# A gather list whose empty places point past the end of the table

## The reference

```
xn  = layernorm(x)
h   = xn @ W
AHW = segment_sum(edge_weight[:, None] * h[dst], src, num_segments=12500)
x   = x + AHW + b + linear_attention(xn)
x   = x + mixture_of_experts(layernorm(x))     # 8 experts, the best 2 for each node
```

## Time and profile before

| | |
|---|---|
| median of 3 runs | 3717.16 us (3711.85 to 3720.75) |
| profiled execution | 3712.03 us |
| its span, first to last instruction | 3710.3 us |
| POOL's gathers at L770 | 1616, 1549.9 us busy |
| HBM read, written | 376.35 MB, 111.03 MB |

### The profile page before, as it was taken

How to read it: one execution, slowest core, us unless ns; L and a number is a source line. 1 busy time by engine, 2 the same in 40 slices (tenths; PEclk the granted TensorE clock), 3 DMA queues, 4 the chain that set the end, 5 groups by cost and what they waited for, 6 DMA issues and landing times. The chain is left out here.

```text
span 3710.3 us, 69265 instructions
## 1 busy us (share of the span) xinstructions
PE 2723.5 (73%) x16161; PEld 2235.5 (60%) x16165; DVE 2553.0 (69%) x6668; ACT 628.5 (17%) x1326; POOL 2548.0 (69%) x2390
## 2 busy tenths in 40 slices
PE   1447776577777777676676667667767999999998
PEld 1346666366566665555555555555533788888887
DVE  9999999455555555677777777777768566654444
ACT  8312222411111111000000000000013221112221
POOL 7347777677777777777777777777745477775444
PEclk9987777789999999888899898998877999999999
DMA  5545555634444444444444444444457455555443
GB/s 173 167 144 183 180 184 158 222 117 128 127 125 128 125 124 126 131 131 125 131 131 131 129 127 131 131 131 124 125 177 220 73 115 114 112 114 92 73 75 52
DMA packets 327621, 492.01 MB, mean 133 GB/s; under 512 B 60714, under 2 KB 247854, under 8 KB 327214
## 3 DMA queue, kind: packets, MB, share of 16 engines
q0 software_dynamic: 127584, 270.17, 28.9%
q1 hardware_dynamic: 161029, 176.37, 15.6%
q10 hardware_dynamic: 38601, 41.04, 3.5%
HBM read 376.35 MB, written 111.03 MB: 131 GB/s over the span
## 5 line engine op out<-in xcount | busy, mean ns | idle before, releaser
L770 POOL DMA_INDIRECT message<-h_table,records x1616 | 1549.9, 959 | 511.5 <-issue 498.4
L1278 PE MATMUL bank<-message,select 128*128 128x256 f32 x3232 | 924.5, 436 | 566.7 <-issue 296.6
L1278 PEld LDWEIGHTS bank<-message,select 128*128 128x128 f32 x3232 | 665.4, 215 | 781.7 <-issue 404.2
L1821 DVE TENSOR_SCALAR select<-iota_n,records 128x128 f32<-128x128 f32 x1660 | 594.3, 358 | 501.4 <-PE bank L1278 486.9
L1829 DVE TENSOR_TENSOR acc<-acc,bank 128x256 f32 x1660 | 683.4, 412 | 9.9 <-PE bank L1278 6.0
L823 POOL DMA_INDIRECT out<-acc,row_of x210 | 331.7, 1580 | 302.5 <-DVE acc L2356 152.5
L735 POOL DMA_INDIRECT lists<-placed,dest_i x300 | 348.5, 1162 | 201.2 <-ACT placed L957 106.9
L1514 PE MATMUL bank<-w,acc 128*128 x1680 | 387.1, 384 | 19.7 <-DVE acc L2340 19.7
L1501 PE MATMUL bank<-fx_t,acc 128*128 128x256 f32 x1680 | 380.1, 379 | 2.5 <-ACT fx_t L1096 2.5
L1514 PEld LDWEIGHTS bank<-w,acc 128*128 128x128 f32 x1680 | 315.6, 193 | 61.5 <-issue 21.5
L1501 PEld LDWEIGHTS bank<-fx_t,acc 128*128 128x128 f32 x1680 | 318.7, 190 | 46.0 <-ACT acc L1103 1.9
(11 more groups left out here) (356 smaller groups left out, 3579.2 us busy)
## 6 DMA issues: line engine op xcount, KB each, us to landing
fetched<-h_table SPq DMA_DIRECT2D x3200, 1.0 KB
fetched<-h_table ACTq DMA_DIRECT2D x2432, 1.0 KB
rows<-block_dram SPq DMA_DIRECT2D x75, 514.5 KB
acc<-x_sorted SPq DMA_DIRECT2D x105, 260.0 KB, 3.1
message<-h_table,records POOLq DMA_INDIRECT x1616
xt_in<-xt_dram SPq DMA_DIRECT2D x98, 256.0 KB
lists<-zeros_list SPq DMA_DIRECT2D x8, 1664.0 KB, 14.9
read_back<-lists SPq DMA_DIRECT2D x13, 1024.0 KB, 7.0
```

Of the source, the lines that this page charges most:

```text
L770: pool.indirect_dma_start(out=message[:, k % SETS, j, :], out_offset=None, in_=h_table, in_offset=Offset(ap=records[:, k * SET + j, 0:1], ...
L1278: last = nc.tensor.matmul(ps, select[:, slot % 2, j, :], rows_of, start=True, stop=True)
L1821: return V.tensor_scalar(select[:, k % 2, j, :], iota_n[:, :], records[:, k * SET + j, 1:2].bitcast(F32), records[:, k * SET + j, 2:3].bit ...
```

## The change

The number that marks a place without an edge is now 16,384 (`ABSENT`), past the last row of `h_table`, and every gather gets a bound, 12,543, with rows above it to be skipped. `message` is zeroed once, so that a slot that has never been written holds zeros; later a skipped place keeps what an earlier set left there, and its weight of 0 takes it out. The row numbers of the tiles that SP and ACT fetch are cut off at 12,543, since those transfers have no bound. The column `lane` and its iota go.

```diff
--- before.py
+++ after.py
@@ -91,6 +91,8 @@
     PAD = 1 << 14
     assert NB * 2 * (G8 - 1) + CG <= SLOTS and K % STEP == 0 and NCOL >= NGP and M % 5 == 0 and TAIL_REST
     SET, SETS, RING = 4, 4, 8
+    ABSENT = 1 << 14
+    assert ABSENT >= NB * P
     TT = -(-((NG * P + NB * (P - 1)) // P) // SET) * SET
     RSEG = -(-TT // P)
     TC = RSEG * P
@@ -250,7 +252,7 @@
         row_ok = sb("row_ok", [P, 2, P], F32, early)
         w_nat = sb("w_nat", [P, 8, C], F32, early)
         message = sb("message", [P, SETS, SET, C], F32, early)
-        lane = sb("lane", [P, 1], F32, early)
+        absent = sb("absent", [P, 1], F32, early)
         select = sb("select", [P, 2, SET, P], F32, early)
         fetched = sb("fetched", [P, 2, 2, C], F32, early)
         fetch_f = sb("fetch_f", [P, FETCHED], F32, early)
@@ -748,7 +750,8 @@
             steps.settle()
             pool.engine_nop().then_inc(s_late, 1)
             pool.iota(iota_n[:, :], [[1, P]], base=0, channel_multiplier=0, allow_small_or_imprecise_dtypes=True)
-            pool.iota(lane[:, :], [[1, 1]], base=0, channel_multiplier=1, allow_small_or_imprecise_dtypes=True)
+            pool.memset(absent[:, :], float(ABSENT))
+            pool.memset(message[:, :, :, :], 0.0)
             steps.done(pool.memset(head_mask[:, :], 1.0))
             steps.done(pool.memset(row_ok[:, :, :], 1.0))
             steps.settle()
@@ -769,7 +772,8 @@
                 for j in range(SET - (k in fetched_of)):
                     pool.indirect_dma_start(
                         out=message[:, k % SETS, j, :], out_offset=None, in_=h_table,
-                        in_offset=Offset(ap=records[:, k * SET + j, 0:1], axis=0)).then_inc(s_message[k % SETS], 16)
+                        in_offset=Offset(ap=records[:, k * SET + j, 0:1], axis=0),
+                        bounds_check=NB * P - 1, oob_is_err=False).then_inc(s_message[k % SETS], 16)
             for k in range(TSETS):
                 pool.wait_ge(s_records, part_of(k))
                 if k >= SETS:
@@ -1879,7 +1883,7 @@
                 steps.done(V.tensor_tensor(records[:, part, 2], fb, fa, ALU.bitwise_or))
                 steps.settle()
 
-                steps.done(V.tensor_scalar(fa, records[:, part, 2].bitcast(F32), 0.0, lane[:, 0:1], ALU.is_equal, ALU.mult))
+                steps.done(V.tensor_scalar(fa, records[:, part, 2].bitcast(F32), 0.0, absent[:, 0:1], ALU.is_equal, ALU.mult))
                 steps.settle()
                 V.tensor_tensor(records[:, part, 0], records[:, part, 0], fa, ALU.max).then_inc(s_records, 1)
                 if nth == 0:
@@ -1896,8 +1900,10 @@
                 for k in (range(1, 3), range(3, 6), range(6, 7), range(0))[nth]:
                     set_turn(k)
             dve.wait_ge(s_records, len(PARTS))
-            steps.done(V.tensor_copy(fetch_f[:, 0:SP_FETCHED], records[:, SP_TILE:SP_TILE + (SP_FETCHED - 1) * SP_SPAN * SET + 1:SP_SPAN * SET, 0]))
-            steps.done(V.tensor_copy(fetch_f[:, SP_FETCHED:FETCHED], records[:, ACT_TILE:ACT_TILE + (ACT_FETCHED - 1) * ACT_SPAN * SET + 1:ACT_SPAN * SET, 0]))
+            steps.done(V.tensor_scalar(fetch_f[:, 0:SP_FETCHED], records[:, SP_TILE:SP_TILE + (SP_FETCHED - 1) * SP_SPAN * SET + 1:SP_SPAN * SET, 0],
+                                       float(NB * P - 1), None, ALU.min))
+            steps.done(V.tensor_scalar(fetch_f[:, SP_FETCHED:FETCHED], records[:, ACT_TILE:ACT_TILE + (ACT_FETCHED - 1) * ACT_SPAN * SET + 1:ACT_SPAN * SET, 0],
+                                       float(NB * P - 1), None, ALU.min))
             steps.settle()
             V.engine_nop().then_inc(s_fetch_f, 1)
             for k in range(RING - 1, RING):
```

## The result

The changed kernel takes 3,798.3 us (median of 4 runs, 3,789.95 to 3,804.63) against 3,714.5 of the kernel before in the same comparison: a ratio of 1.0228, with a 95% interval of 1.0205 to 1.0251. It is slower, by 84 us where 53 were forecast. The profiled execution has a span of 3,796.7 us, 86.4 more than before.

A forecast was written before the change was run, and what follows sets the result against it. POOL's gathers were taken to bound the stage. The profiled 3,712.0 us plus 53 for the bound and 0 for the rest gave 3,765, with 5 us more 3,770 us as a median; range for 8 in 10: 3,635 to 3,960.

The forecast's parts named there:

- What bounds the stage: POOL's 1,616 gathers at L770 set the pace, 1.268 us each; a nanosecond per gather is 1.616 us of the kernel.
- The bound's price: Each gather at L770 compares 128 row numbers with a bound: 33 ns taken, 53 us in all; high end 1,012 us.
- The rows skipped: 12,094 absent places in POOL's gathers needn't be written: between nothing and 89 us saved, nothing taken into the forecast.
- The middle bound: POOL's time per skipped row, from the accumulating scatter's extra 626 ns for 128 rows: 4.9 ns each, 59 us in all.
- The operand: An extra instruction per gather on POOL's sequencer for the bound: hidden, cost 0; uncovered, 17 ns each, 27 us.
- The memset: Zeroing `message` once on POOL before the first gather: 3.5 us, covered by 8.5 us of waiting, cost 0.
- Skipping pays: Rival at L770: bound free, 4.9 ns saved per absent row, 47 us in all, 3,670 us; chance 0.34.
- Nothing changes: Rival at L770: bound compared at no cost, skipped rows still written out in some form, 3,717 us; chance 0.20.
- A pass of its own over the rows: Rival at L770: the check adds 150 to 626 ns per gather, 3,959 to 4,729 us; chance 0.07.
- The sign: Direction of the whole kernel's change: slower 0.46, the same 0.20, faster 0.34.

The follow-up runs named there:

- the shorter list: The kernel before with `TT` smaller by 36 tiles, 35 of them gathered by POOL and all empty on these inputs: 3,667.9 us, ratio 0.9887.
- the run with one move: The changed kernel with the bound moved into a register once ahead of the gathers, instead of once for each of the 1,616: 3,798.8 us, ratio 1.0245.

## Why the prediction was right, and where it was off

*What bounds the stage.* Right. 55.7 ns more per start make 90.0 us over 1,615 steps, the shorter list gave 44.7 us where 44 were expected, and the gathers of 64 and 32 rows took 72 and 122 us off the kernel, where 46 and 83 ns a gather make 74 and 134. With 32 rows the stage of the profile is 127 us shorter (2614.8 - 693.1 against 2,048.3) and the part behind it 10 us longer, which is within what that part varies by.

*The bound's price: the mis-sized term.* I took 33 ns, from the scatter at L805 as the nearest row. The bound alone measures 53, the changed kernel 56. The direction was right for the reason given, extra work in every gather. The size came from a row that has nothing to do with checking, the difference between two directions of transfer; that it lies within a factor of two is luck. With 56 ns in its place the sum is 3,717 + 90 = 3,807, 9 us above the 3,798 measured. 3 of them are the kernel before, which has 3,714.5 in this comparison; the rest lies within what the part behind the last gather varies by. What the work is stays open: the runs show that a bound lengthens each gather whether or not a row is skipped, and without the moves, but they don't separate the comparing of 128 row numbers from whatever else the instruction does when it has a bound.

*The rows skipped.* Nothing was taken for them and nothing came: 998 ns with half of all rows skipped. The middle bound, 4.9 ns per row from the accumulating scatter, was wrong by four to seven times for a row that the instruction hasn't got (0.7 to 1.2 ns), and altogether for one that it has and skips. The 626 ns of that scatter therefore aren't the price of 128 more rows of this kind; what they are was not tried. The rule of the Trainium skill that was weighed against them ("DMA: Bandwidth & Descriptors", on the anatomy of a DMA on the gpsimd path) agrees with these runs in so far as the cost of one row more is small: from 32 to 128 rows the gather grows by 83 ns of 946. It shows at each step measured, though, 37 ns from 32 to 64 rows and 46 from 64 to 128.

*The operand.* Right: the moves came, 29 ns each and not 17, and the run with one move shows them hidden. The cover is larger than the two gathers that I read from the earlier trace rows, which say only how long a semaphore instruction stands open: the last move leads its gather by 12.5 us.

*The memset.* Right, a little dearer: 4.36 us instead of 3.5. (The cover was 12.23 - 3.5 = 8.7 us by the numbers given, not 8.5.) The timeline of the kernel after:

```profile
678.97 4.36 POOL L754 MEMSET message<- 128x4096 f32 x1
...
684.47 0.31 POOL L764 TENSOR_SCALAR_AFFINE_SELECT head_mask<-head_mask 128x128 f32<-128x128 f32 x1
...
689.13 0.60 ACT L1019 ACTIVATE found<-bank 128x512 bf16<-128x512 f32 x1
689.83 0.25 DVE L1871 TENSOR_SCALAR records<-found 128x128 int32<-128x128 int32 x1 [9.95 <-ACT found L1019]
...
693.50 1.08 POOL L773 DMA_INDIRECT message<-h_table,records  x1 [8.72 <-DVE records L1888]
```

POOL still waits 8.72 us for DVE's records (12.23 in the earlier trace rows), and DVE starts them behind ACT's copy and not behind POOL; the first gather is 0.4 us later, of which 0.3 were there at ACT's copy of the found words already (689.13 against 688.83).

*The rivals.* Skipping pays: fallen, by the run with half of the rows skipped. Nothing changes: fallen. A pass of its own over the rows, from 150 ns: fallen, at 56. The sign was given a chance of only 0.46 because the rival that skipping pays rested on the 4.9 ns; even with the 1.2 ns of a row left out of the instruction its gain could have been no more than 12,094 x 1.2 = 15 us, less than half of the 53 us that I gave the bound, and the run with half of the rows skipped shows none.

## What to carry to other kernels

Ask first whether a transfer's bytes or its issue set the pace: here POOL needed 1.25 us to issue a gather whose data kept the DMA engines 43% busy, so bytes saved were worth nothing and 56 ns added to each issue were worth 90 us. The indirect DMA on POOL had a price here that goes mostly by the instruction: rows skipped in it didn't shorten it, half as many rows took 5% off it (900 for 946 ns), and an instruction left out gave back all of its time, about 1.3 us. When a price is bounded by the rows of another form of an instruction, say what that form does differently: the 626 ns of an accumulation told nothing of the price of a row.

## What the runs showed that was not expected

Skipped rows take no packet away: with half of the rows skipped the software queue has the same 127,584 packets and 111 MB fewer bytes, and the page counts 27,188 more packets under 512 B than that of the kernel before (87,902 against 60,714). 111 MB are some 108,500 rows, so there is about one small packet for four skipped rows. The check that reports an error is dearer than the one that skips silently, 1,012 against 999 ns, although no row was past the bound in either. And the page's line of HBM traffic read 376.35 MB in all three, the kernel before, the changed one and the one with half of the rows skipped; gathers of 64 rows brought it to 270.44. Of skipped rows only the queue's line tells: its time falls from 28.9 to 19.2% of the span with half of them skipped, about as far as with gathers of 64 rows:

```profile
q0 software_dynamic: 101728, 164.26, 21.0%
```
